# Three attentions on one core: row maxima taken four units ahead instead of three, and projections of the second attention from its third batch on in three fp16 passes

## The reference

```python
x = x + L0_xattn(ln(x), ctx, mask0, position_bias)     # 16 heads of 64
x = x + L0_ffn(ln(x))                                  # 16 experts, 4 chosen
x = x + L1_xattn(ln(x), ctx, ctx, mask1, bias1)        # 16 heads of 8
x = x + L1_ffn(ln(x))
x = x + L2_xattn(ln(x), ctx, ctx)                      # retention
x = x + L2_ffn(ln(x))
x = x + L3_xattn(ln(x), ctx, ctx, mask of ones)        # 16 heads of 8
x = x + L3_ffn(ln(x))

# L1_xattn, per head (L3 the same without bias and without masked keys)
q, k, v = ln(x) @ Wq.T + bq, ctx @ Wk.T + bk, ctx @ Wv.T + bv
scores = q @ k.T / sqrt(8) + bias1
scores = where(mask1 == 0, -inf, scores)
out = softmax(scores) @ v @ Wo.T + bo
```

## Time and profile before

| what | value |
|---|---|
| median of three runs | 1470.1 us (1463.5 to 1475.24) |
| the profiled execution | 1461.97 us |
| its span, first to last instruction | 1460.2 us |
| mean granted clock of PE | 0.956 of full speed |
| busy share of the span | PE 90%, PEld 55%, DVE 71%, ACT 62%, POOL 63% |
| wide attention | about 20 to 370 us |
| second attention | about 745 to 985 us |
| third softmax attention (layer 3) | about 1247 to 1436 us |

### The profile page before, as it was taken

One profiled execution on the slowest core, in us unless ns is written; L12 is line 12 of the kernel. 1 busy time (PEld: TensorE's weight loads), 2 busy tenths in 40 slices (PEclk: granted clock), 3 DMA queues, 4 the chain that ended last, 5 costly groups with the idle time before them and its releaser, 6 DMA issues.

```text
span 1460.2 us, 37325 instructions
## 1 busy us (share of the span) xinstructions
PE 1318.7 (90%) x14582; PEld 807.8 (55%) x14582; DVE 1039.4 (71%) x2493; ACT 899.9 (62%) x1487; POOL 913.2 (63%) x879
## 2 busy tenths in 40 slices
PE   5999999997979999999979999986989799799987
PEld 3466566665757777777743433433567466344435
DVE  7888888888744344444647989986698477677775
ACT  4677787774859999999934544432234332465556
POOL 6788887876658999899857646522262120655535
PEclk9899999999989999999968999997989899799999
DMA  8000000000013110000101021000000000000000
GB/s 276 9 9 9 9 9 9 2 2 17 29 34 100 60 34 29 29 29 14 67 4 33 34 66 33 31 2 29 1 2 3 8 1 1 8 9 5 5 2 30
DMA packets 26083, 39.64 MB, mean 27 GB/s; under 512 B 7314, under 2 KB 13365, under 8 KB 25429
## 3 DMA queue, kind: packets, MB, share of 16 engines
q1 hardware_dynamic: 25364, 35.58, 7.5%
q0 software_dynamic: 576, 2.10, 0.7%
HBM read 38.72 MB, written 1.05 MB: 27 GB/s over the span
## 4 chain that ended last, share of the span: by engine, by line
PE 59%; DVE 25%; POOL 6%; issue 5%; ACT 4%; DMA 1%; SPq 0%; POOLq 0%; DVEq 0%; ACTq 0%
PE bank L1870 11%; PE bank L1811 10%; DVE sbuf L920 6%; PE bank L757 3%; PE bank L2336 2%; DVE sbuf L330 2%; PE bank L1264 2%; PE bank L709 2%; PE bank L1368 2%; PE bank L2094 2%; POOL sbuf L1216 2%; DVE sbuf L937 2%; PE bank L1296 2%; PE bank L1345 2%; PE bank L2315 2%
## 5 line engine op out<-in xcount | busy, mean ns | idle before, releaser
L1821 ACT ACTIVATE sbuf<-bank,sbuf 128x512 f32<-128x512 f32 (+1 forms) x512 | 323.1, 684 | 30.2 <-PE bank L1811 18.1
L1841 POOL TENSOR_TENSOR sbuf<-sbuf 128x512 f16<-128x512 f32 x256 | 304.9, 1199 | 56.4 <-ACT sbuf L1821 55.2
L1870 PEld LDWEIGHTS bank<-sbuf 128*128 128x128 f16 x3072 | 194.1, 98 | 67.4 <-issue 7.7
L1870 PE MATMUL bank<-sbuf 128*128 128x128 f16 x3072 | 214.4, 220 | 6.4 <-DVEq L1958 6.4
L310 POOL TENSOR_TENSOR sbuf<-sbuf 128x2 f32<-128x2 f32 (+1 forms) x48 | 39.7, 827 | 285.0 <-DVE sbuf L305 280.1
L1811 PE MATMUL bank<-sbuf 128*128 128x512 f16 x768 | 209.1, 382 | 0.0
L920 DVE TENSOR_REDUCE sbuf<-bank 128x4 f32<-128x1024 f32 x128 | 156.4, 1222 | 57.1 <-PE bank L709 42.2
L1953 DVE SCALAR_TENSOR_TENSOR sbuf<-bank,sbuf 128x128 f32<-128x128 f32 x256 | 71.7, 342 | 166.2 <-PE bank L1870 165.9
L1216 POOL TENSOR_TENSOR sbuf<-sbuf 128x512 f16<-128x512 f32 x128 | 147.9, 1176 | 57.1 <-ACT sbuf L1463 57.0
L757 PE MATMUL bank<-sbuf 128*32 128x256 f32 x2048 | 140.5, 394 | 1.6 <-ACT sbuf L857 1.6
L1210 POOL TENSOR_TENSOR sbuf<-sbuf 128x512 f16<-128x512 f32 x96 | 111.3, 1175 | 23.0 <-ACT sbuf L1451 22.9
(11 more groups left out here) (319 smaller groups left out, 2736.9 us busy)
## 6 DMA issues: line engine op xcount, KB each, us to landing
sbuf<-w SPq DMA_DIRECT2D x32, 256.0 KB, 2.9
sbuf<-bias_t SPq DMA_DIRECT2D x4, 1024.0 KB, 12.3
sbuf<-ctx_t SPq DMA_DIRECT2D x24, 128.0 KB, 2.4
sbuf<-bias_q POOLq DMA_DIRECT2D x4, 512.0 KB, 11.4
sbuf<-mask_t SPq DMA_DIRECT2D x8, 256.0 KB, 2.7
sbuf<-bias_t SPq DMA_DIRECT2D x8, 256.0 KB, 3.0
sbuf<-mask_q SPq DMA_DIRECT2D x8, 256.0 KB, 3.6
sbuf<-bias_q SPq DMA_DIRECT2D x8, 256.0 KB, 4.2
```

Of the source, the lines that this page charges most:

```text
L1821: last = act.activation(to, bank[u % 4][:, :], ACT.Gelu, bias=b1[u // U][:, u % FT0:u % FT0 + 1], scale=1 / SCALE)
L1841: g.tensor_tensor(hid16[1][:, u % BUFS, :], hid[:, u % 4, :], hid16[0][:, u % BUFS, :], ALU.subtract)\
L1870: last = pe.matmul(bank[4 + out_no % 2][:, j * P:(j + 1) * P], hid16[h][:, u % BUFS, j * P:(j + 1) * P], w2_16[p][:, w, f * D:(f + 1) * D] ...
```

## The change

Two edits. The first is in all three attentions: AHEAD becomes 4. Before the loop there are still three scores (range(AHEAD - 1)); at u = 0 the loop issues scores(3) and scores(4), and after that scores(u + 4), on PE and on DVE. So DVE's cut moves from even u to odd u, and maxima(Q) on PE stays where it was.

The second is in the second attention: batches 0 and 1 are projected in fp32 as before, batches 2 to 7 (FIRST16 = 2) in three fp16 passes. The fp16 copies of the inputs have one buffer (RING16 = 1), those of layer 3 two. On POOL, weights16 comes at b == 1 after all fp32 projections are done, inputs16(b + 1) at b = 1 to 6 after masks_beside(b, 1), and lead.weights moves from b == 1 to b == 2. PE waits for sixteen before the first job of a batch from batch 2 on. SCALE is 256 for both, and ACT divides by it only where the job was in fp16. The constant scale_col is set at the start. LOADS of the retention goes from 2 to 1: its context comes in one DMA instead of two, on one semaphore instead of two.

```diff
-            PER_BATCH, AHEAD = PAIRS, 3
+            PER_BATCH, AHEAD = PAIRS, 4
...
+            if masked:
+                w16 = [take([2, HG * P], F16), take([2, HG * P], F16), take([2, D], F16)]
+                x16, c16 = [take([2, S], F16)], [take([2, S], F16)]
+            else:
...
+            FIRST16, RING16 = 2 * masked, len(x16)
+            SCALE = 2.0 ** 8
...
+            def scored_at(u):
+                return [w for w in ((AHEAD - 1, AHEAD) if u == 0 else (u + AHEAD,)) if w < B * PER_BATCH]
...
# inputs16 on POOL
-                wait(g, s["projected"], JOBS * (b - 1))
+                wait(g, s["projected"], JOBS * (b - RING16 + 1))
...
# POOL's loop
+                    if masked and b == 1:
+                        g.wait_ge(s["projected"], FIRST16 * JOBS)
+                        weights16(g)
+                    if FIRST16 <= b + 1 < B:
                         inputs16(g, b + 1)
-                    if gated and b == 1:
+                    if gated and b == 2:
                         lead.weights(g)
...
# project on PE
-                        if not masked:
+                        if b >= FIRST16:
                             pe.wait_ge(s["sixteen"], halved16(b))
...
-                            if masked:
+                            if b < FIRST16:
                                 last = pe.matmul(to[:, c * S:(c + 1) * S], (wq, wk0)[kind][:, m, :],
                                                  ct if kind else xt, start=True, stop=True)
                                 continue
                             for n, (w, half16) in enumerate(PASSES):
...
# loops of PE (the same on DVE, and in the wide attention)
-                for u in range(AHEAD):
+                for u in range(AHEAD - 1):
                     scores(u)
                     if u == 1:
                         maxima(0)
...
-                    if u + AHEAD < B * PER_BATCH:
-                        scores(u + AHEAD)
+                    for w in scored_at(u):
+                        scores(w)
...
# DVE
-                        if (u + AHEAD) % 2:
-                            cut((u + AHEAD) // 2)
+                    for w in scored_at(u):
+                        scores(w)
+                        if w % 2:
+                            cut(w // 2)
...
# wide_attention
-            JOBS, QK, NP, AHEAD, BEHIND = 12, 8, PAIRS, 3, 2
+            JOBS, QK, NP, AHEAD, BEHIND = 12, 8, PAIRS, 4, 2
...
# retention
-            LOADS = 2
+            LOADS = 1
```

More of the change, by code:

```diff
@@ L524, in narrow_attention @@
                 "hidden_keys",
-            ) if k not in (("sixteen",) if masked else ("masks", "biased", "hidden_keys"))}
+            ) if masked or k not in ("masks", "biased", "hidden_keys")}
             ctx_in = [sem(L + f"ctx_in{p}") for p in range(2)]
@@ L697, in project @@
                             for n, (w, half16) in enumerate(PASSES):
[L698 removed]
+                                last = pe.matmul(o, c16[b % RING16][:, half16, t * P:(t + 1) * P], w16[2][:, w, :],
                                                  start=t == n == 0, stop=t == 1 and n == 2, skip_group_check=True)
@@ L830, in project @@
                     src = job_bank(b, k)
+                    unit = 1 / SCALE if b >= FIRST16 else 1.0
                     if k < QK:
@@ L836, in project @@
                             last = act.activation(x32[:, k % 2, c * S:(c + 1) * S], src[:, c * S:(c + 1) * S], ACT.Identity,
-                                                  bias=bias, scale=(DH ** -0.5 if kind == 0 else 1.0) / SCALE)
+                                                  bias=bias, scale=unit * (DH ** -0.5 if kind == 0 else 1.0))
                     else:
@@ L844, in project @@
                                 src[:, t * D:(t + 1) * D].rearrange("p (g j d) -> p g j d", j=HG, d=DH), ACT.Copy,
-                                scale=1 / SCALE)
+                                scale=unit)
                     last.then_inc(s["evacuated"], 1)
@@ L1124, in wait_pr_free, with scored_at @@
                         pe.wait_ge(x_done, x0 + SB * b + k + 1)
+            def scored_at(u):
+                return [w for w in ((AHEAD - 1, AHEAD) if u == 0 else (u + AHEAD,)) if w < UNITS]
             def heads_of(n):
@@ L1384, in tensor @@
                         scores(0)
-                for u in range(1, AHEAD):
+                for u in range(1, AHEAD - 1):
                     scores(u)
@@ L1397, in tensor @@
                         maxima(u // 2 + 1)
-                    if u + AHEAD < UNITS:
-                        scores(u + AHEAD)
+                    for w in scored_at(u):
+                        scores(w)
                     if u >= BEHIND:
```

16 lines of the change are left out of this document (6 added, 10 removed).

## The result

| | before | after |
|---|---|---|
| median (runs) | 1467.54 us (11) | 1484.54 us (11) |
| lowest and highest | 1462.84, 1475.24 us | 1474.08, 1487.25 us |
| profiled execution, its span | 1461.97, 1460.2 us | 1486.19, 1484.4 us |
| mean granted clock | 0.956 | 0.936 |

The changed kernel is slower by 0.8%: ratio 1.0082, 95% interval 1.0058 to 1.0105 (taken over all runs; the medians alone are 17.0 us apart). The forecast was 1459 us, with a range of 1446 to 1474.

A forecast was written before the change was run, and what follows sets the result against it. PE was taken to bound the wide and layer 3 attentions, PE or DVE in turn the second. Terms of -4.9, -3.5 and -2.3 us sum to -10.7, factor 0.9927, forecast 1459 us, range 1446 to 1474.

The forecast's parts named there:

- In the loop this adds and removes no instruction: Attention loops: same scores and reductions; the cut comes two units before its transposes, so PE doesn't wait for it.
- The cut waits: All three attentions: PE's idle before L725 and L1306 on DVE falls from 30.3 to about 8 us.
- Wide attention: Waits of PE removed, -6.8 us, and the fill, +1.9 us, sum to -4.9 us.
- rival B: Cut wait becomes a reduction wait, DVE fills up, fills and POOL's work eat the rest: 1470 us; chance 0.15.
- The fill: At u = 0 scores(4) precedes batch 1's projections and waits for unit 3's reduction: +1.9 wide, +2.0 second, +1.7 layer 3.
- Layer 3: Its attention, bound by PE: waits removed, -4 us, and the fill, +1.7 us, sum to -2.3 us.
- Cut: Second attention: PE's shorter waits for the cut save 0.4 us a batch, -3 us over eight.
- fp16: Second attention, projections of six batches: 1.0 us saved a batch, -6 us, bounds 0 and -8.4.
- inputs16 on POOL: Second attention: 2.1 us a batch, hidden in POOL's 7.08 us idle before power; collisions with DVE +2 us over six.
- weights16 and the later lead.weights: Second attention, POOL: +1 us for delays and +1.5 us for a second collision with DVE's small operations.
- C: POOL's new work collides with DVE's small operations, 23 us at two cuts a batch: +17 us, 1487 us; chance 0.07.
- D: Shared lock: each of 24 inputs16 instructions blocks a DVE operation 0.5 us, +12 in place of +2: 1469 us; chance 0.08.

The follow-up runs named there:

- scale_first: Changed kernel with DVE's layer-norm scale at n = 1 put ahead of the reduction in the narrow attentions; 1465.1 us, ratio 0.9974 to the kernel before.
- even_cut: Changed kernel with DVE's cut held back to even u, ahead of that unit's reduction; 1474.0 us, ratio 1.0018 to the kernel before.
- ahead_only: Changed kernel with fp32 projections throughout the second attention and lead.weights back at b == 1; 1473.38 us, ratio 1.0024 to the kernel before.
- best: scale_first with the wide attention back at three units ahead; 1457.08 us, ratio 0.9912 to the kernel before.
- best_fp32: best with fp32 projections in the second attention and lead.weights back at b == 1; 1458.19 us, ratio 0.991 to the kernel before.
- fp16_only: Changed kernel with AHEAD = 3 and the earlier loops in all three attentions, the rest kept; 1473.56 us, ratio 1.0037 to the kernel before.
- scale_three32: Kernel before, with LOADS = 1 and the layer-norm scale at n = 1 ahead of the reduction in narrow attentions; 1469.99 us, ratio 1.0004.

## Why the prediction was wrong

**The step that failed** is "In the loop this adds and removes no instruction... What moves is that the cut of a quad comes two units before its transposes". The prediction followed the cut to its transposes and not to what it is moved in front of, and put the price of that at nothing. From even to odd units it lands at n = 1 between the reduction and the scale, for which PE's turn waits at n = 2. The kernel's text had it: "at n = 1 DVE scales the layer norm of batch b - 2". scale_first shows it for the narrow attentions, by removing that one order: -19.4 and -4.6 us. even_cut shows it for the wide one, by putting the cut back to even units: -6.0 us.

By stages the sum was off by 13.9 us in the wide attention, by 10.5 in the second and by -0.8 in layer 3.

**The cut waits** fell as said: all of L725 and L1306 on DVE were 30.3 us, those of L736 and L1322 are 6.3 (4.1 + 2.2, the first transposes of the three attentions; about 8 was predicted). The target of the edit was met in full and the time not saved.

**Wide attention:** predicted -6.8 + 1.9 = -4.9, measured +9.0. In place of a saving of 6.8 over eight, 0.85 us a batch, the batch grew by 0.86 us, since the transposes now wait 13.2 us for ACT; that the wait only changed its owner is rival B's mechanism, and that the cut's place decides it is shown by even_cut. The odd cut makes ACT late by way of DVE's bias, as far as the releasers show it. The fill was mis-sized: the first batch is 4.3 us longer. In its first batch PE waits 1.73 us for the reduction of unit 3 at 48.05 us, and the clock is 0.93 in the batch, where it was 0.99: the prediction priced the wait, and no clock behind it.

**Layer 3:** predicted -4 + 1.7 = -2.3, measured -3.1, in the predicted way: steady batches 0.58 us shorter (0.5 predicted), the first 3.2 us longer and the second 1.35 us shorter, where the fill was put at 1.7. scale_first shows that another 4.6 us were there to be had.

**Second attention:** predicted -3.5, measured +7.0.
- Cut, -3 predicted: in ahead_only the batches with full clock are 0.3 us shorter, those with a fall 1.3 us longer.
- fp16, -6 predicted, in bounds of 0 and -8.4: alone it is 0, with the order mended 0.2 us a batch (best against best_fp32) to 0.4 (scale_first against best_fp32), so 1.2 to 2.5 us over six batches, and no gain in the timed runs. "There PE's saving is worth nothing" held for the whole batch and not only for n = 1 and 2.
- inputs16 on POOL is hidden, as said: PE never waits for sixteen, and the gap before power is 4.6 us (7.08 before, about 5 predicted). weights16 and the later lead.weights: +2.5 predicted; fp16_only's first two batches are +2.0.
- The fill: predicted +2.0; the wait is 1.32 us (at 770.66, for unit 3's reduction), where 1.5 was predicted. The first two batches are +3.0 us in the changed kernel and +1.2 in ahead_only, which has the same order: in the right size, and no better known than the clock allows.
- The price of the moved order stood in no term: in a steady batch PE waits 1.14 us longer for the scale, and the clock behind that wait costs some 1.6 us (as in ahead_only), against all that the two edits save.

**The rivals.** B named what became of the gain, without its loss. C had the right side and the right meeting, a small DVE operation beside POOL, but hung it on the new POOL instructions, and that its 1487 us lies near the measured 1484.54 is luck; in the event it is the old masks and splits that the moved cut and scale meet, and the price is paid by the scale's reader. Its 23 us are not there: DVE's busy time in a batch is 26.24 us in fp16_only and 26.00 before. The same 0.24 us rules out D, for which it had to be 2. By the rule of the Trainium skill (SBUF — State Buffer, "Who interferes with whom") a DVE operation can block when it takes the shared port pair. The trace agrees for operations on SBUF alone: in the batch shown L939 takes 0.73 us and L941 0.97, where such a pair took 0.18 and 0.20 in the earlier trace rows, and the PSUM readers keep 1.20 to 1.23 us here too.

Two of the prediction's own signs came: "or if a clock drop appears where there is none now", and DVE's operations of the cut grew in total, from 41.0 us (L927 and L929) to 49.3 (L939 and L941), while L330 fell from 70.9 to 65.3. By the 1.6 us that a fall costs in ahead_only, the steady batches would be about 27.3 us without it (28.90 - 1.6, an estimate), which is what was predicted for them; no run shows it. One number of its chances is a slip: 0.2 and a fifth of 0.5 are 0.30, not 0.32.

## What to carry to other kernels

When an instruction is moved in an in-order queue, list what it is moved in front of and who waits for that, just as for what it leaves; here a cut of 0.4 us (1.7 beside POOL) in front of a scale cost more than the waits it removed. Before work is taken off one engine, look whether the order of the other makes it wait: here 1.25 us less of PE's work a batch gave nothing alone, and at most 0.4 us with the order mended. Put the step whose reader is waiting ahead of the one whose reader comes later. Running one unit further ahead paid in the steady state of the narrow attentions, where the order on DVE was right, hardly in the wide one (0.13 us a batch in even_cut), and it cost in the first batch of each; that a later start of it helps isn't shown.

## What was not expected of the hardware

A single wait of PE of 1.3 to 2.1 us in otherwise busy code can be followed by about 4 us at 0.57 of the clock: in the second attention behind waits of 2.13 us four times in four, of 1.77 us twice in four, of 1.30 us twice (even_cut), of 1.29 us once (fp16_only), of 0.99 us never. The longest single wait is not all of it: in best a wait of 1.75 us (at 826.30) has no fall behind it, and in scale_three32 the clock falls at 1427 us with no single wait over 1.06 us before it. A fall costs 1.6 us, nearly as much as the wait.

What PE takes for a stretch of identical code differs by 7% between the profiled executions of two kernels (93.0 and 99.8 us busy), and repeats to 0.2 us in a second profiled execution of each. The cause is open.
